# Row maxima as 48-row products in the two halves of the array, expert numbers loaded once and a tile ahead

## The reference, cut to what matters

```python
q = q * hd ** (-0.5)                                   # 32 score heads, hd = 8, T = 2048
att = jnp.einsum('bhtd,bhsd->bhts', q, k) * (1.0 / math.sqrt(hd))
att = jnp.where(causal, att, -jnp.inf)
att = jax.nn.softmax(att, axis=-1)                     # needs the maximum of each row
att = att[:, :, 0] - lambda_full * att[:, :, 1]        # pairs of score heads

g = jnp.einsum('bh,ehm->bem', xt, gate_proj_w)         # 8 experts, 256 -> 512
u = jnp.einsum('bh,ehm->bem', xt, up_proj_w)
h = jax.nn.silu(g) * u
eo = jnp.einsum('bem,emh->beh', h, down_proj_w)        # 512 -> 256
combined = jnp.einsum('beh,be->bh', eo, c)             # c: two experts per token
```

## Time and profile before

| | |
|---|---|
| median of three executions | 3425.56 us (3422.33 to 3430.25) |
| the profiled execution | 3424.31 us, its span 3422.6 us |
| mean granted clock of TensorE | 0.975 of full speed |
| busy: PE, VectorE, ScalarE, GpSimd | 3190.5, 2799.1, 2306.1, 1617.0 us |
| the experts' stage | 325 to 741 us of the span |
| products psM of line 1078 in it | 320 |
| masks of line 1084 in it | 88 |
| maxima of line 1002 in it | 280 |

### The profile page before, as it was taken

One profiled execution on the slowest core, in us unless ns is written; L12 is line 12 of the kernel. 1 busy time (PEld: TensorE's weight loads), 2 busy tenths in 40 slices (PEclk: granted clock), 3 DMA queues, 4 the chain that ended last, 5 costly groups with the idle time before them and its releaser, 6 DMA issues. The chain is left out here.

```text
span 3422.6 us, 60314 instructions
## 1 busy us (share of the span) xinstructions
PE 3190.5 (93%) x19844; PEld 1290.6 (38%) x19844; DVE 2799.1 (82%) x4898; ACT 2306.1 (67%) x3660; POOL 1617.0 (47%) x2112
## 2 busy tenths in 40 slices
PE   7997999969999999999999999769999999999987
PEld 4654666642222222222222222343333334333333
DVE  6766677758889888888888888258898989898997
ACT  4444333328888888888888888657777767778763
POOL 2113400003444444344444444207788888887885
PEclk9999999989999999999999999989999999999998
DMA  5352311111111111111011110142222222222221
GB/s 169 129 157 85 77 60 52 49 52 34 55 39 40 45 37 34 33 33 35 28 39 32 36 31 17 40 141 59 66 75 80 69 74 69 75 84 69 75 78 50
DMA packets 163277, 213.87 MB, mean 62 GB/s; under 512 B 34213, under 2 KB 110253, under 8 KB 162973
## 3 DMA queue, kind: packets, MB, share of 16 engines
q1 hardware_dynamic: 141340, 172.51, 16.3%
q0 software_dynamic: 10880, 20.73, 2.0%
q10 hardware_dynamic: 10752, 16.78, 1.5%
HBM read 156.45 MB, written 52.69 MB: 61 GB/s over the span
## 5 line engine op out<-in xcount | busy, mean ns | idle before, releaser
L1481 ACT ACTIVATE prob<-psS 128x1024 f32<-128x1024 f32 (+3 forms) x1280 | 1092.6, 907 | 262.3 <-PE psS L1676 251.4
L1531 DVE TENSOR_REDUCE pmax<-psR 128x1 f32<-128x512 f32 x1512 | 961.5, 684 | 143.9 <-PE psR L1612 94.0
L2318 POOL TENSOR_TENSOR hc<-h_d,crep 128x512 f32<-128x512 f32 x512 | 647.0, 1271 | 188.8 <-DVE h_d L2547 138.3
L1691 PE MATMUL psVo<-prob,vaug 128*32 128x512 f32 (+3 forms) x5120 | 628.9, 545 | 2.0 <-ACT ov L1485 0.9
L1612 PE MATMUL psR<-kslab,qslab 48*128 48x512 bf16 (+3 forms) x2240 | 590.6, 349 | 33.2 <-DVE pmax L1531 17.7
L1676 PE MATMUL psS<-qslab,kslab 51*128 51x512 bf16 (+3 forms) x2560 | 531.8, 353 | 42.8 <-ACT prob L1481 26.0
L1395 POOL TENSOR_SCALAR_AFFINE_SELECT prob<-prob 128x256 f32<-128x256 f32 (+1 forms) x512 | 212.0, 419 | 715.5 <-ACT prob L1481 715.3
L2547 DVE TENSOR_TENSOR_SCAN h_d<-a,state,psU 128x512 f32<-128x512 f32 x384 | 489.3, 1275 | 0.0
L2537 DVE TENSOR_TENSOR psU<-dtx,psX 128x512 f32<-128x512 f32 x512 | 356.2, 696 | 92.1 <-PE psX L2697 41.3
L2450 ACT ACTIVATE a<-dt,a_neg 128x512 f32<-128x512 f32 x512 | 366.9, 724 | 54.3 <-DVE h_d L2547 53.4
L1612 PEld LDWEIGHTS psR<-kslab,qslab 48*128 48x128 bf16 x2240 | 166.2, 94 | 560.0 <-DVE pmax L1531 281.3
(11 more groups left out here) (355 smaller groups left out, 5125.5 us busy)
## 6 DMA issues: line engine op xcount, KB each, us to landing
crep<-c_rows_d SPq DMA_DIRECT2D x256, 256.0 KB, 3.1
x_e<-rows_d SPq DMA_DIRECT2D x72, 128.0 KB, 2.0
y_d<-y SPq DMA_DIRECT2D x72, 128.0 KB, 1.7
q_d<-parts SPq DMA_DIRECT2D x48, 128.0 KB
k_d<-parts SPq DMA_DIRECT2D x48, 128.0 KB
qslab<-q_d SPq DMA_DIRECT2D x60, 96.0 KB
kslab<-k_d SPq DMA_DIRECT2D x60, 96.0 KB
wg<-n_L_ffn_gate_proj_w_dram ACTq DMA_DIRECT2D x8, 512.0 KB, 4.3
```

The costliest lines, as they stand in the source:

```text
L1481: act.activation(prob[g % BUFS][:, :, off:BLK], psS[g % 2][:, :, off:BLK], ACT.Exp).then_inc(prob_ready, 1)
L1531: dve.tensor_reduce(into[:, lo:lo + (count - 1) * NEXT + 1:NEXT], psR[at % BANKS][:, 0:count * w].rearrange("p (n w) -> p n w", w=w), AX.X ...
L1691: ins = pe.matmul(psV[lo:lo + VW, off:BLK], vaug[n % 2][:, st, :], prob[g % BUFS][:, a, off:BLK], start=(st < 2), stop=(st >= TPB * c + TP ...
L2318: pool.tensor_tensor(hc[:, g % CR], h[:, g % HR], crep[:, g // PAIR % SPR], ALU.mult).then_inc(hc_ready, 1)
```

## The change

Two things are done in phase_experts.

The buffers qz go. Queries of all four pairs are loaded into slabs with both heads (qearly: the two qslabs and two new buffers qmore), and a product of maxima takes only the 48 rows of its head, both of queries and of keys. The loads into qz, their four memsets and the waits of GpSimd for max_full go with them; the counts of early_in and early_made are made to fit. The mask product stays as it is.

The expert's number is loaded once for each tile, between the up and the down products: step i loads number[i+1], step i+1 uses it for the gate and up products and step i+2 for the down products.

```diff
-        MADE = 2 * RING + 8
+        MADE = 2 * RING + 4
+        KM = 6 * HD
...
-        qz = [[sb(f"qz{u}{a}", [P, T], BF16) for a in range(2)] for u in range(2)]
+        qmore = [sb(f"qmore{u}", [P, T], BF16) for u in range(len(EARLY_HEADS) - SLABS)]
+        qearly = qslabs + qmore
...
-            return 384 + 96 * (j + 1 + max(j - 1, 0))
+            return 384 + 192 * max(j - 1, 0)
...
-            for u in range(2):
-                for a in range(2):
-                    c.after(pool.memset(qz[u][a][:], 0.0))
-
             def load_queries(j):
                 for a in range(2):
                     row, lo = 2 * EARLY_HEADS[j] + a, HALF * a
                     for at_, count, part in ((0, 3, 0), (3, 2, 1), (5, 1, 2)):
-                        pool.dma_start(qz[j % 2][a][lo + at_ * HD:lo + (at_ + count) * HD, :],
+                        pool.dma_start(qearly[j][lo + at_ * HD:lo + (at_ + count) * HD, :],
                                        q_rows[row, part].unsqueeze(0).to_broadcast([count, HD, T])).then_inc(early_in, 16)
...
-            load_queries(0)
             c.after(pool.memset(ident_m[:], 0.0))
...
-            pool.wait_ge(early_in, loads_done(0))
-            load_queries(1)
             for j in range(2, len(EARLY_HEADS)):
                 pool.wait_ge(early_in, loads_done(j - 1))
                 load_keys(j)
-                pool.wait_ge(max_full, NITEM * (j - 1) + CREDIT)
                 load_queries(j)
...
-                    bank = psM[at_ % MAX_BANKS]
+                    bank, rows = psM[at_ % MAX_BANKS], slice(HALF * a, HALF * a + KM)
                     for m, (i_, ch, w) in enumerate(parts):
-                        ins = pe.matmul(bank[:, m * w:(m + 1) * w], qz[j % 2][a][:, i_ * P:(i_ + 1) * P],
-                                        kearly[j][:, ch * BLK:ch * BLK + w], start=(m == 0), stop=not masked,
+                        ins = pe.matmul(bank[:, m * w:(m + 1) * w], qearly[j][rows, i_ * P:(i_ + 1) * P],
+                                        kearly[j][rows, ch * BLK:ch * BLK + w], start=(m == 0), stop=not masked,
                                         skip_group_check=True)
...
+            number = {}
...
                 if known(i, 0):
-                    e = pe.value_load(at(keep["table"][0:1, 0], i), min_val=0, max_val=E - 1)
+                    e = number[i]
                     pe.wait_ge(xTl_ready, i + 1 + CREDIT)
...
+                if known(i + 1, 0):
+                    number[i + 1] = pe.value_load(at(keep["table"][0:1, 0], i + 1), min_val=0, max_val=E - 1)
                 if known(i - 1, 0):
-                    e = pe.value_load(at(keep["table"][0:1, 0], i - 1), min_val=0, max_val=E - 1)
+                    e = number.pop(i - 1)
                     pe.wait_ge(hTl_ready, i + CREDIT)
...
                 if n < SLABS:
-                    pe.wait_ge(keep["early_in"], 384 + 96)
+                    pe.wait_ge(keep["early_in"], 384)
```

## The result

The changed kernel takes 3455.88 us (median of four executions, 3452.49 to 3456.4) against 3424.05 us before: a ratio of 1.0087, 95% interval 1.0074 to 1.0100. It is slower by 0.9%, 32 us, where 21 were forecast.

What follows compares the result with a forecast made beforehand. PE's instruction stream was taken to bound the experts' stage: 3424.3 + 28.9 (boundaries 41.3 less overlap 12.4) - 7.2 (start) - 0.8 (expert number) = 3445.2; stated as 3446 us, range 3436 to 3459.

Steps and rivals of the forecast that it cites:

- What bounds the stage: Experts' stage: PE's instruction stream alone sets the time; pitches sum to 365.2 us at full clock, stretch 367.8.
- The sign named for it: Profile after, 400 to 700 us: PE 100% busy, tiles 6.0 us instead of 5.55, last product of maxima at 758.
- Part 2, the start: Ahead of the first maxima: dropping zeroed buffers removes a 4.9 us wait and 2.3 us of slow clock, -7.2 us.
- Part 3, the expert's number: PE's loads of the expert number: 72 fewer gain only where the queue ran empty, at early tiles, -0.8 us.
- Part 1, overlap: Products of maxima in places with two items: neighbours in opposite array halves run side by side, saving 12.4 us.
- third rival: Products of maxima: pairs don't overlap because the second's weights wait for its PSUM bank; +33.3, 3457.6 us; chance 5%.
- Part 1, the price of a boundary: Experts' stage: 444 passages between 48-row and whole-array products at 93 ns each cost 41.3 us.
- The first, a boundary that costs nothing: Experts' stage: next weights load into the idle half, so passages are free; 3404 us; chance 5%.
- The second, only one side paid: Experts' stage: one side of each passage is hidden by the queue, 20.6 us paid, 3424.5 us; chance 4%.
- The fourth, a falling clock: PE: drains lower the granted clock, 5% less over 395 us is +20 us, 3465; chance 4%.

Runs made afterwards that it cites:

- b_start: Kernel before, zero buffers kept but zeroed by VectorE in the first four tiles, so first queries and constants load earlier; 128-row products; 3416.5 us, 0.9980.
- b_both: Kernel before with the earlier start (VectorE zeroes the buffers) and the expert's number loaded once, a tile ahead; products keep 128 rows; 3415.8 us, 0.9982.
- b_number: Kernel before with only the expert's number loaded once, a tile ahead; 3426.8 us, 1.0008.
- b_rows112: b_both with products of maxima over rows 0 to 111 instead of 0 to 127; 3420.7 us, ratio 0.9984 to the kernel before.

## Why the prediction held, point by point

**What bounds the stage**: right. PE's instruction stream is the time; the sum of pitches fits (365.2 forecast without the slow clock, 365.5 in b_start and b_both, which have none in the stretch). The sign named for it came, a little larger: a tile takes 6.10 us (6.0 forecast), and the last product of maxima starts 29.7 us later than before, at 766.7, not 21.

**Part 2, the start**: right to a few tenths. -5.7 us ahead of the maxima and -2.3 inside are -8.0, which with part 3's first tiles is what was forecast (-7.2 and -0.8). Constants are ready at 357.7 (356 forecast) and asked for at about 365. b_start shows this part alone.

**Part 3, the expert's number**: right. b_number shows nothing that the median can tell, and no hole in the dense stretch.

**Part 1, overlap**: right. All 58 pairs start 3 to 4 ns apart; the 58 places that could overlap take 20.0 us instead of 26.2, and with the ways out of them taken off (58 x 0.102 = 5.9) that is the 12.4 of the forecast to 0.3 (11.9 when each start is compared with its own in b_both). So the third rival (no overlap) has not come, although its 3457.6 us lies nearest to the measured time. This is a case where the time alone would have picked the wrong story; the x2 rows tell it.

**Part 1, the price of a boundary**: the mechanism was right, the term was mis-sized, and 7 of the 10 us that the forecast lacks lie in it. It said 93 ns with the same on both sides, so 41.3 us. The stretch says 401.47 - 365.52 = 35.9 net, and with the forecast's 12.4 of overlap 48.3 us, 109 ns for each of the 444. By starts, the changed kernel against b_both, which has the same products in the same order: in, 96 ns (312 against 216, 205 against 109), near the forecast. Out, 102 ns (317 to 319 against 216, and 266 against 163 into a mask). Behind the way out another 10 ns for the next product, some 178 times, and for the second of two turns 57 ns, 44 times. Above the forecast's price that makes 222 x 3 ns + 222 x 9 ns + 178 x 10 ns + 44 x 57 ns = 6.9 us of the 7.0 that are missing. The rows for it were there. Rows 6 gave 0.32 against 0.21 for the way out, and I took the middle of both sides; over all 69 such ways out of a 512-column maximum into a turn in the attention stage of before the median is 317 ns, so "90 to 100 ns" was low there too. And the turns behind a half-array product have a first pitch of 165 instead of 109 ns, 123 times in the same trace.

**The rest of the miss**, from 28 us of the stage to 32 of the medians, is inside the interval of the ratio (25 to 34 us) and in stages that vary by themselves; no run here assigns it.

**The rivals that were not near.** The first, a boundary that costs nothing, fell: the runs have 109 ns where it needed under 46. The second, only one side paid, fell with it: 96 ns in, 102 out. The fourth, a falling clock, fell too: 1.00 throughout.
The Trainium skill's "up to 2x" for a dimension of 64 or less (TensorEngine Tiling (Array Packing), Theoretical Speedup), taken for every maximum, did not come: overlap gives 11.9 us and the boundaries take 48. The same page's sentence that a change of the tiling mode drains the engine (Key Properties) agrees with these runs, which show the cost and not its inside. b_rows112 agrees as well: 112 rows behave as the whole array does.

## What to carry to other kernels

In this kernel products over half the rows saved nothing singly and gained only in pairs; each passage between half-array and whole-array products cost about 0.1 us on either side of them, plus a little behind. So count the passages before the rows, put all half-array products of a step together, and keep their masks in the same half. And when a helper's setup stands ahead of the bound engine's first need, move the setup first, as a change of its own: here that gain (8 us, b_both) was real in both forms, and hidden in a change that lost 36 beside it.

## What was not expected of the hardware

After leaving the half-array form, not only the first but the second whole-array product is late: by 10 ns for 16-bit weights, by 57 ns for the second of two 32-bit turns. And a product of 112 rows costs no passage, but has a pitch of 219 to 220 ns at 512 columns where 128 rows have 215 to 216 ns.
